# A state-space block with a binary MLP on one core: statistics of the first phase two batches ahead, and one difference moved from GpSimd to VectorE

## The reference

```python
xn = layernorm(x)
# attn(xn): B, T, D = 8, 512, 128; E = 256, N = 64
normed = rmsnorm(xn, input_norm_w)
x_z, z = split(normed @ in_proj_W)
xc = silu(conv4_depthwise(x_z) + conv_b)
dt = clip(softplus(xc @ dt_W + dt_b), 0.001, 0.1)
Bp, Cp = xc @ B_W, xc @ C_W
for t in range(T):                       # the scan
    h = exp(dt[t] * A) * h + dt[t] * Bp[t] * xc[t]
    y[t] = (h * Cp[t]).sum(n)
y = y * silu(z)
x1 = xn + y @ out_proj_W
attn = x1 + (silu(n2 @ gate_W) * (n2 @ up_W)) @ down_W     # n2 = rmsnorm(x1)
# ffn(xn): three layers with weights +1 / -1
out = x + attn + ffn(xn)
```

## Time and profile before

| what | us |
|---|---|
| median of 3 runs | 1098.99 |
| lowest, highest | 1097.1, 1102.58 |
| profiled execution | 1097.32 |
| its span in the trace | 1095.5 |

### The profile page before, as it was taken

One profiled execution on the slowest core, in us unless ns is written; L12 is line 12 of the kernel. 1 busy time (PEld: TensorE's weight loads), 2 busy tenths in 40 slices (PEclk: granted clock), 3 DMA queues, 4 the chain that ended last, 5 costly groups with the idle time before them and its releaser, 6 DMA issues.

```text
span 1095.5 us, 28254 instructions
## 1 busy us (share of the span) xinstructions
PE 956.2 (87%) x8006; PEld 424.3 (39%) x8006; DVE 915.3 (84%) x2035; ACT 922.9 (84%) x1125; POOL 847.7 (77%) x1216
## 2 busy tenths in 40 slices
PE   5988883568999999997999997999999899999898
PEld 3565541113434343433433332433333334343436
DVE  5677673998989999997999997898998899998992
ACT  1656776899989999997999997899997999999981
POOL 6555523888888888886888887898887798988880
PEclk9999986999999999998999999999999899999999
DMA  5245359999999999997899999898989799989940
GB/s 156 102 163 183 145 215 358 353 345 354 343 349 334 347 355 354 358 348 309 337 357 352 347 348 343 296 346 345 367 323 371 260 363 355 363 334 373 374 150 11
DMA packets 81004, 333.74 MB, mean 305 GB/s; under 512 B 15152, under 2 KB 35504, under 8 KB 45488
## 3 DMA queue, kind: packets, MB, share of 16 engines
q1 hardware_dynamic: 80688, 331.11, 81.8%
q10 hardware_dynamic: 128, 0.49, 0.1%
HBM read 306.38 MB, written 25.17 MB: 303 GB/s over the span
## 4 chain that ended last, share of the span: by engine, by line
PE 34%; DVE 26%; POOL 20%; issue 14%; ACT 3%; DMA 1%; DVEq 1%; ACTq 0%; SPq 0%; POOLq 0%
POOL decayed L623 14%; PE ps L828 11%; DVE ps L1259 8%; PE ps L773 7%; DVE state L1270 6%; PE ps L913 6%; PE ps L927 4%; DVE h L1367 2%; DVE soft L1185 2%; POOL soft L573 1%; PE ps L891 1%; PE ps L899 1%; PE ps L696 1%; ACT state L1061 1%; DVE gated L1332 1%
## 5 line engine op out<-in xcount | busy, mean ns | idle before, releaser
L623 POOL TENSOR_TENSOR decayed<-decay,state 128x256 f32<-128x256 f32 x1024 | 725.4, 733 | 152.5 <-DVE state L1270 103.9
L1041 ACT ACTIVATE decay<-decay,a_col 128x2048 f32<-128x2048 f32 x256 | 514.0, 2008 | 26.2 <-issue 17.9
L1270 DVE TENSOR_TENSOR state<-decayed,ps 128x256 f32<-128x256 f32 x1024 | 407.5, 418 | 58.8 <-POOL decayed L623 41.2
L1259 DVE TENSOR_TENSOR ps<-decay,ps 128x512 f32<-128x512 f32 x512 | 352.8, 689 | 41.1 <-ACT state L1061 16.0
L828 PE MATMUL ps<-state,c_cols 128*32 128x256 f32 x4096 | 336.8, 402 | 0.0
L1061 ACT COPY state<-ps 128x512 f32<-128x512 f32 x512 | 287.8, 587 | 54.7 <-issue 37.4
L773 PE MATMUL ps<-moving,b_rows 64*128 64x256 bf16 x1024 | 204.0, 280 | 89.9 <-DVE ps L1259 86.6
L780 PE MATMUL ps<-moving,b_rows 64*128 64x256 bf16 x1024 | 205.1, 282 | 13.0 <-DMA b_rows<-b_stage 13.0
L913 PE MATMUL ps<-h,w 128*128 128x256 f32 x512 | 176.8, 432 | 0.8 <-DVE h L1367 0.8
L773 PEld LDWEIGHTS ps<-moving,b_rows 64*128 64x128 bf16 x1024 | 58.4, 95 | 262.9 <-DVE ps L1259 163.7
L828 PEld LDWEIGHTS ps<-state,c_cols 128*32 128x32 f32 x4096 | 82.1, 110 | 112.3 <-issue 103.2
(11 more groups left out here) (124 smaller groups left out, 813.2 us busy)
## 6 DMA issues: line engine op xcount, KB each, us to landing
decay<-dt_stage SPq DMA_DIRECT2D x512, 512.0 KB, 6.3
moving<-u_stage SPq DMA_DIRECT2D x63, 256.0 KB
u_stage<-u_parts SPq DMA_DIRECT2D x16, 512.0 KB, 2.8
b_rows<-b_stage SPq DMA_DIRECT2D x63, 128.0 KB
b_stage<-b_parts SPq DMA_DIRECT2D x16, 384.0 KB, 3.3
dt_stage<-dt_tok SPq DMA_DIRECT2D x8, 512.0 KB, 3.1
moving<-u_stage SPq DMA_DIRECT2D x126, 32.0 KB
x_tok<-in_L_attn_x_dram SPq DMA_DIRECT2D x4, 512.0 KB, 4.0
```

The lines of the kernel that those rows point to most:

```text
L623: nc.gpsimd.tensor_tensor(decayed[:, p], decay[:, dec_slot(m, k), p, k % TS, :], state[:, (k - 1) % RING, p * E:(p + 1) * E], ALU.mult).th ...
L1041: nc.scalar.activation(pair, pair, ACT.Exp, scale=a_col[:, 2:3]).then_inc(decay_ready, 1)
L1259: nc.vector.tensor_tensor(ps[:, acc_bank(m, k), :].rearrange("p (q e) -> p q e", q=HQ), decay[:, dec_slot(m, k), HQ:Q, k % TS, :], ps[:, a ...
L1270: nc.vector.tensor_tensor(state[:, k % RING, p * E:(p + 1) * E], decayed[:, p], ps[:, SELFP + k % 2, p * E:(p + 1) * E], ALU.add).then_inc ...
```

## The change

Three edits in phase 1. On VectorE `moments` moves from the first place of a round to the place before `dt_and_u`, and works for batch s + 2 instead of s + 1; batch 0's statistics are written out ahead of the rounds. On GpSimd `log_err` is gone. On VectorE the difference, which stood there for the last batch alone, is now done for every batch, right behind its sum.

```diff
@@ gpsimd @@
-                def log_err(q, bb):
-                    n = q * 2 + bb
-
-                    if n == B - 1:
-                        return
-                    after(pool, "p_ready", n)
-                    after(pool, "dt0_ready", n, back=1)
-                    nc.gpsimd.tensor_tensor(soft[:, 2], soft[:, 2], soft[:, 1], ALU.subtract
-                                            ).then_inc(S["log_err_ready"], 1)
@@ gpsimd, slot @@
                     at(norms, 1)
                     at(first_rest, -2)
-                    at(log_err, -1)
                     at(second_rest, -2)
@@ vector, exp_to_p @@
                     nc.vector.tensor_scalar(soft[:, 2], soft[:, 1], 1.0, -1.0, ALU.add, ALU.add
                                             ).then_inc(S["p_ready"], 1)
-                    if n == B - 1:
-                        after(dve, "p_ready", n)
-                        nc.vector.tensor_tensor(soft[:, 2], soft[:, 2], soft[:, 1], ALU.subtract
-                                                ).then_inc(S["log_err_ready"], 1)
+                    after(dve, "p_ready", n)
+                    nc.vector.tensor_tensor(soft[:, 2], soft[:, 2], soft[:, 1], ALU.subtract
+                                            ).then_inc(S["log_err_ready"], 1)
@@ vector, slot @@
-                    at(moments, 1)
                     at(first_rests, -2)
                     at(dt_bias, -1)
                     at(normalize, 1)
                     at(b_to_sbuf, -1)
                     at(exp_to_p, -1)
                     at(second_rests, -2)
+                    at(moments, 2)
                     at(dt_and_u, -1)
@@ vector @@
+                moments(0, 0)
                 batches(dve, slot, prepare_scan)
```

## The result

The changed kernel takes 1089.93 us, the median of 8 runs (1084.88 to 1092.12), against 1098.05 us (8 runs, 1094.36 to 1102.58) for the kernel before beside it. The ratio is 0.9931, with a 95% interval of 0.9908 to 0.9955. Its profiled execution took 1092.12 us, the longest of the eight; the span in its trace is 1090.0 us.

The account below looks back on a forecast made before the run. TensorE with its hand-over was to set the round at 15.54 us instead of the statistics' chain at 17.33 us; seven intervals of 108.7 to 109.1 us against 116.98 us save 8.1 us, giving 1090 us (range 1086.5 to 1096.5).

Parts of the forecast that it names:

- the statistics' string: Phase 1's chain per batch: statistics on VectorE, then `norms`, `u_rest` and on to `u_tok`; 17.33 us a batch.
- First interval: From the first `dt` product (L709) to the second; the second at 37.91 instead of 38.66 us, so 15.44 us.
- The hand-over: From the end of TensorE's convolution through ScalarE's silu to the next `dt` product: 0.87 us a batch.
- The lower end of the unknown: Silu hand-over to TensorE of 0.7 us, as two silus of 1.26 us suggest: gain 9.3 us.
- VectorE's round: VectorE's work per batch in phase 1, `u_tok` ending at +18.06 us: hidden, about 0.5 us ahead of Exp.
- the bounds 1.23 and 3.03 us: Length of the difference on VectorE: 1.23 us alone, 3.03 us beside GpSimd's L591; 3.03 us was taken.
- L573's 2.48 us and a hand-over go: Moving GpSimd's difference (L573) to VectorE takes its 2.48 us and one hand-over off phase 1's chain.
- Case B: Rival: VectorE late behind Exp, GpSimd's third part of `u` blocks `exp_to_p`; 0.8 us a round, 1095 us; chance 0.15.
- the point of decision: In `exp_to_p`: VectorE more than 0.25 us behind Exp lets GpSimd's L591 go first.
- Case C: Rival: loads or scan behind phase 1 do not move with it, swallowing the gain; 1098 us; chance 0.06.
- D: Rival, GpSimd's seam between rounds: `norms` ends 5.0 us after `u_tok`; 0.45 us more a round, 1102 us; chance 0.05.
- The later marks: Signs of being right: `xc_feat` wait about 0.5 us, last L709 near 131 us, scan's first product near 174, scan 913 us.

Follow-up runs that it names:

- the two kernels with halves: `dt` products started on the first half of `xc_feat`, in the changed kernel (ratio 0.9903, 1086.82 us) and in the kernel before (0.9988, 1097.27 us).
- the short pad: Changed kernel with one unused VectorE sum over 768 numbers ahead of `exp_to_p` in every round: ratio 0.9929, 1088.99 us.
- the statistics alone: Kernel before with only the statistics moved two batches ahead, the difference left on GpSimd: ratio 0.9906, 1087.45 us.
- the difference alone: Changed kernel with the statistics put back to the round's start, so only the difference on VectorE remains: ratio 0.9983, 1095.04 us.
- the long pad: Changed kernel with two unused VectorE sums over 768 numbers ahead of `exp_to_p` in every round: ratio 1.0047, 1101.60 us.
- the kernel with three taps: Changed kernel with one of the convolution's four taps left out, 12 matmuls a round instead of 16: ratio 0.9965, 1093.24 us.
- the changed kernel again: Changed kernel measured once more with no edit, against the kernel before: ratio 0.9932, 1090.01 us.
- the 16 `memset`s: 16 one-number VectorE instructions added behind phase 1, in the changed kernel (ratio 0.9971, 1095.72 us) and in the kernel before (1.0029, 1100.58 us).

## Why the prediction was right, point by point

The measured 1089.93 us stands against 1090 us forecast. That the two agree to 0.1 us is luck: the rounds gave 0.9 us more than was taken, the ratio's own interval is 2.6 us to either side, and the parts around the rounds scatter by more than the difference (first convolution by 1.6 us, scan 913.1 against 915.3 us in the two profiles). What is no luck is the round and where its time went.

**The bound.** Right: the statistics' string was the bound, and TensorE with the silu's hand-over took over. The chain after shows it, the two kernels with halves prove it (14.83 us after the change, 17.35 us without it), and the short pad shows that VectorE isn't the bound.

**First interval.** 15.44 us predicted, 15.36 us measured.

**The hand-over.** The term that was mis-sized. It was put at 0.87 us, from the first round. In later rounds it is 84.70 (end of L670) to 85.47 us, 0.77 us. The silu of the second half starts 0.03 to 0.04 us behind the convolution and takes 0.69 us in both places; the 0.1 us lies between its end and the `dt` product, 0.14 us in the first round and 0.05 us later. For batch 0 alone the code has one more wait there, for the weights; that this is the cause isn't shown. So the first round was the wrong one to take the term from. 0.1 us in seven intervals is 0.7 us: hence a sum of 108.01 us instead of 108.7 to 109.1 us, and a gain of 8.97 us for the 8.1 us taken. The lower end of the unknown (0.7 us, gain 9.3 us) was the nearer one; worked through the prediction's own sum, 0.7 us would give 9.5 us, and the measured 0.77 us gives 9.0 us.

**VectorE's round.** `u_tok` ends at +17.98 us, predicted +18.06. `norms` ends at 74.58 - 54.59 = +19.99 us, predicted +20.5. The estimate for `norms` beside L1172 was too dear by half a microsecond, and so VectorE is 1.02 us ahead of Exp and not 0.5 us.

**The difference.** 3.03 us beside L580, and 1.20 us for its user: both durations as predicted, and of the bounds 1.23 and 3.03 us the right one was taken. By the rule of the Trainium skill ("SBUF — State Buffer", Who interferes with whom) the blocked time goes to whoever issues second; the rows of four kernels agree (3.03 us after, 3.07 us with the statistics alone, 2.50 and 2.55 us in the two that came late).

**What the difference was worth.** Wrong, though the sum doesn't show it. The prediction wrote that on the chain "L573's 2.48 us and a hand-over go", as part of what makes VectorE's round fit. They need not go: with the difference on GpSimd `u_tok` ends at +17.99 us. What was overlooked is that the statistics, moved, fill more than half of the time in which VectorE would wait for L573 (1.27 us, with 1.12 us of waiting left), and that the blocked operation is there either way. The time was worked out for the two halves together, and no sentence asked what each does alone.

**Case B.** A real mechanism with the right price: 0.8 us a round predicted, 0.8 us (the difference alone) and 0.9 us (the long pad) measured. The margin was larger than thought: VectorE has 1.02 us to Exp, to which the prediction adds 0.25 us to the point of decision; a pad of 0.94 us is free and one of 1.80 us is not, and in the difference alone 0.42 us of lateness is too much, so the point lies between 0.03 and 0.42 us behind Exp, around the 0.25 us predicted. In the rounds the long pad leaves a gain of 3.6 us, where case B has 3.4 us. What its price misses is the rest: the total is some 5 us above the kernel before instead of 3.4 us below it, and the profiles put 5 us of that in the scan.

**Case C, D.** C doesn't happen: the scan's first product moves by 7.69 us with phase 1 (182.38 to 174.69 us). D's price was added up a little high (17.76 us a round and 2.6 us in all give 1101 us from the base that the other cases use). Its seam between two rounds on GpSimd is half there, as the timeline of GpSimd after shows:

```profile
69.53 1.09 POOL L552 TENSOR_TENSOR nrm<-mean_var,eps_t 128x4 f32<-128x4 f32 x1 [2.69 <-DVE mean_var L1117]
...
74.16 0.42 POOL L564 TENSOR_TENSOR nrm<-nrm 128x4 f32<-128x4 f32 x1
74.53 2.13 POOL L572 TENSOR_TENSOR u_rest<-u_tok,u_parts 128x1024 f32<-128x1024 f32 x1
```

L552, on 4 numbers a row, takes 1.09 us where it took 0.20 us, since it runs beside L1172 (69.37 to 70.56 us). `norms` ends at 74.58 us and `u_rest` (L572) follows without a wait, though ScalarE's cast was done at 73.69 us: the mark "`u_rest` waiting for the cast and not for `norms`" is wrong, and `norms` is still the last thing ahead of it, by 0.9 us. What the prediction lists as a sign of being wrong, "`norms` still the last thing ahead of `u_rest`", is there, in a kernel whose rounds came out as forecast. The sum had it so (`norms` to +5.0, then `u_rest`), the list of marks contradicted the sum. `norms` ends 2.0 us behind `u_tok`, well short of the 5.0 us from which D would decide. VectorE doesn't idle for `x_tok` once after the first load.

**The later marks.** The wait for `xc_feat` is 0.34 us, where about 0.5 us was named. The last `dt` product near 131 us: 131.80 and 130.44 us in the two profiles. The scan's first product near 174 us: 174.69 and 171.63 us. The scan 913 us: 915.3 and 914.9 us.

## What to carry to other kernels

Before a sum for a change of two parts is believed, work out each part alone: here the statistics' move gave all 9 us of the rounds, and the move of a 2.5 us operation off GpSimd gave nothing behind it, since the engine that would have waited had other work for much of that time. When VectorE and GpSimd meet on operations like these (two inputs in SBUF, or the `tensor_scalar` of `exp_to_p`), ask who issues first and by how much; the price of coming second is a jump (here 1.8 us on one instruction, 0.9 us a round) and it is worth knowing the margin in tenths of a microsecond. And once a chain has gone over to TensorE, look at how it takes its input: splitting one hand-over in halves brought another 0.6 us a round, which would have brought nothing while another engine set the pace.

## What the runs showed of the hardware beyond that

- **Behind a wait of 1.75 us TensorE can run at a lower granted clock, and doesn't always.** In the kernel with three taps five of the eight products took 5.63 us behind waits of 1.75 to 2.19 us, and one took 4.11 us behind the same 1.75 us; in the windows shown the granted clock is 0.70 and 1.00. In the kernel before with halves the two products of 5.6 us stand behind waits of 1.73 and 1.78 us, and the others, behind 0.80 us or less, take 4.0 to 4.1 us. In the kernel before a wait of 2.23 us left the product at 4.11 us, and in the long pad one of 1.68 us did. What decides isn't shown by these traces.
- **The first convolution takes 8.57 to 10.17 us in the same code.** In windows of 2 us from 12.8 us on the granted clock is 1.00 throughout (the expectation of the changed kernel again speaks of the lower clock level; the record of the clock doesn't show it). The windows hold 3, 4, 3, 6 and 5 of its matmuls in the changed kernel's first profile, and 2, 5, 6, 6 and 2 in its second (one that crosses an edge counts in both): the longer execution comes to the quicker pace 2 us later. It moves the whole of phase 1 by up to 1.6 us. As the same kernel gave 10.07 and 8.58 us, no edit is needed for it.
- **The scan's length scatters between 910.4 and 921.5 us in the profiles** of kernels whose scan is the same. That is more than all that the change brought in phase 1, and sets what a measurement of this kernel can tell.
- **A kernel's longer executions are those with the lower mean granted clock of TensorE.** Among the 22 executions of the kernel before beside "after, again", the shortest (1093.51 us) has a mean clock of 0.972 and the longest (1102.37 us) one of 0.953. Taken within each kernel, over all executions on record, 0.01 less of mean clock goes with 4 us more (correlation -0.8). That the clock is the cause isn't shown. It doesn't account for the 16 `memset`s: the mean clock is 0.961 in the kernel before without them and 0.960 with them.
